# Expert rows with their last 64 channels at both ends, transposed two tiles together

## What is computed

```python
def _L0_ffn_ref(x, gate_w, gate_b, w1, b1, w2, b2):       # 4 experts, 2 of them per token
    probs = softmax(einsum('bsd,de->bse', x, gate_w) + gate_b)
    ...                                                    # mask of the two largest, renormalised
    h = gelu(einsum('bsd,edh->ebsh', x, w1) + b1, approximate=False)     # 192 -> 768
    y = einsum('ebsh,ehd->ebsd', h, w2) + b2                             # 768 -> 192
    out = einsum('bse,ebsd->bsd', masked, y)

x = x + conv_ref(_ln_c(x), ...)
t = _to_tokens(x)
t = t + _L0_ffn_ref(_ln_t(t), ...)
```

## Time and profile before

| | |
|---|---|
| time, median of 3 runs | 1939.6 us (1937.39 to 1943.02) |
| the profiled execution | 1935.69 us, span 1933.5 us |
| busy share of the span | PE 92%, PEld 76%, DVE 74%, ACT 65%, POOL 60% |
| busy tenths of PE in 40 slices | `5999999999987983989999999999999999999946` |
| the same of DVE | `4988999899885576778787887887866755555622` |
| granted clock of PE in tenths (9 is 90% or more) | `9999999999997986999999999999999999999977` |
| DMA share in tenths | `4464533222314896878888788788787877667869` |

### The profile page before, as it was taken

One profiled execution on the slowest core, in us unless ns is written; L12 is line 12 of the kernel. 1 busy time (PEld: TensorE's weight loads), 2 busy tenths in 40 slices (PEclk: granted clock), 3 DMA queues, 4 the chain that ended last, 5 costly groups with the idle time before them and its releaser, 6 DMA issues. The chain is left out here.

```text
span 1933.5 us, 35208 instructions
## 1 busy us (share of the span) xinstructions
PE 1772.1 (92%) x9644; PEld 1460.3 (76%) x9644; DVE 1428.1 (74%) x3470; ACT 1253.0 (65%) x2481; POOL 1158.6 (60%) x1077
## 2 busy tenths in 40 slices
PE   5999999999987983989999999999999999999946
PEld 3666666666655773878888888888899888889934
DVE  4988999899885576778787887887866755555622
ACT  3888888888864431656666666666667666677822
POOL 3777666766661026777777777777676675444310
PEclk9999999999997986999999999999999999999977
DMA  4464533222314896878888788788787877667869
GB/s 100 148 166 130 154 96 96 86 82 81 99 38 134 269 272 219 259 197 237 247 231 237 224 249 249 198 241 225 220 219 192 251 201 199 164 178 180 236 201 335
DMA packets 246671, 364.51 MB, mean 189 GB/s; under 512 B 27620, under 2 KB 178532, under 8 KB 246436
## 3 DMA queue, kind: packets, MB, share of 16 engines
q1 hardware_dynamic: 186500, 286.26, 48.6%
q0 software_dynamic: 50016, 60.00, 15.2%
q10 hardware_dynamic: 9984, 16.26, 2.4%
HBM read 228.83 MB, written 135.73 MB: 189 GB/s over the span
## 5 line engine op out<-in xcount | busy, mean ns | idle before, releaser
L1395 POOL DMA_INDIRECT acc_scratch<-yo,tix x262 | 432.6, 1651 | 274.9 <-DVE yo L1813 168.1
L1976 PE MATMUL bank<-x_all,w1b 128*128 128x512 f32 (+1 forms) x2100 | 542.8, 388 | 1.0 <-ACT hf L1449 1.0
L1993 PE MATMUL bank<-w_hl,hh 128*128 x1572 | 491.6, 363 | 10.6 <-DVE hl L1928 6.4
L1449 ACT ACTIVATE hf<-bank,b_col 128x512 f32<-128x512 f32 (+1 forms) x420 | 277.8, 661 | 317.9 <-PE bank L1976 316.4
L1928 DVE TENSOR_TENSOR hl<-hf,hh 128x512 fp32r<-128x512 f32 (+1 forms) x420 | 274.1, 656 | 220.9 <-ACT hh L1452 219.7
L1994 PE MATMUL bank<-w_hl,hl 128*128 x1572 | 396.8, 252 | 0.0
L1976 PEld LDWEIGHTS bank<-x_all,w1b 128*128 128x128 f32 x2100 | 352.4, 188 | 49.3 <-ACT hf L1449 1.4
L666 DVE SCALAR_TENSOR_TENSOR bank<-zwin,wdw,bank 128x512 f32<-128x512 f32 (+2 forms) x462 | 336.6, 735 | 49.0 <-PE bank L766 40.4
L1380 POOL DMA_INDIRECT xs_scratch<-xn,idx x256 | 297.7, 1163 | 85.1 <-issue 75.0
L1993 PEld LDWEIGHTS bank<-w_hl,hh 128*128 128x128 f32 x1572 | 296.0, 188 | 51.0 <-issue 18.4
L1994 PEld LDWEIGHTS bank<-w_hl,hl 128*128 128x128 f32 x1572 | 299.7, 191 | 16.9
(11 more groups left out here) (267 smaller groups left out, 2901.3 us busy)
## 6 DMA issues: line engine op xcount, KB each, us to landing
w1b<-w1s_scratch SPq DMA_DIRECT2D x140, 768.0 KB, 4.9
xs<-xs_scratch SPq DMA_DIRECT2D x61, 522.0 KB, 6.0
xtok_scratch<-xtok SPq DMA_DIRECT2D x32, 384.0 KB, 2.9
xtok<-xtok_scratch SPq DMA_DIRECT2D x32, 384.0 KB, 6.9
acc_scratch<-x SPq DMA_DIRECT2D x32, 384.0 KB, 6.3
xn<-acc_scratch SPq DMA_DIRECT2D x32, 384.0 KB, 5.7
xc_a<-in_x_dram SPq DMA_DIRECT2D x32, 256.0 KB, 2.7
out_dram<-xs ACTq DMA_DIRECT2D x32, 256.0 KB, 4.7
```

Of the source, the lines that this page charges most:

```text
L1395: nc.gpsimd.indirect_dma_start(acc_dram, bass.IndirectOffsetOnAxis(ap=tix[:, J % 4, t:t + 1], axis=0), yo[:, J % YN, t, :], None, compute_ ...
L1449: nc.scalar.activation(hf[:, k % 3, 0:cols], lb[k % 2][:, 0:cols], ACT.Gelu, bias=b1_col[:, bass.ds(exp_of[J] * CH + k, 1)]).then_inc(gelu, 1)
L1976: last = nc.tensor.matmul(lb[k % 2][:, 0:cols], w[:, q, :], v[:, J % 2, 0:cols], start=(i == 0), stop=(i == 4))
L1993: nc.tensor.matmul(out[:, 0:2 * C], hh[:, k % 3, cols], w, start=(k == 0), stop=False, skip_group_check=True)
```

## The change

The row is laid out anew: the last 64 channels, token number, four gate weights, then all 192 channels (`C0` on). It begins and ends with the same 64 channels and still has 261 numbers. So in a partition of `xs` the end of tile `2a` and the beginning of tile `2a + 1` are 128 neighbouring columns, and one transpose turns the last channels of both: those of the even tile land on partitions 0 to 63, those of the odd one on 64 to 127. `mb[1]` is thus half as wide. ScalarE writes the high part of each half on its own partitions, with one copy for even and one for odd tiles; VectorE writes the rest of each on the other 64 partitions, also in two instructions. Even tiles have the high part on top and odd ones at the bottom, which is the same to the weights.

```diff
-CID, CG = 2 * CA, 2 * CA + 1
-CW = CG + E
+CID, CG = CB, CB + 1
+C0 = CG + E
+CW = C0 + C
...
+            def c_turned(m, t):
+                return mb[1][CB * t:CB * t + CB, 0:64 * m].rearrange("p (a n) -> p a n", n=128)
+            def c_part(J, rows, t):
+                return x_c[rows * CB:rows * CB + CB, J % 2, 0:128 * tiles(J)].rearrange("p (a t n) -> p a t n", t=2, n=128)[:, :, t, :]
...
@@ ScalarE, k == 2
                             act.wait_ge(ac2, 2 * nxt + 2)
-                            nc.scalar.activation(x_c[:, nxt % 2, 0:cols], mb[1][:, 0:cols], ACT.Copy).then_inc(hi2, 1)
+                            for t in (0, 1):
+                                last = nc.scalar.activation(c_part(nxt, t, t), c_turned(tiles(nxt), t), ACT.Copy)
+                            last.then_inc(hi2, 1)
...
-                            nc.scalar.activation(xn[:, s % XN, :, C:CID], xn[:, s % XN, :, CA:C], ACT.Copy)
+                            nc.scalar.activation(xn[:, s % XN, :, 0:CB], xn[:, s % XN, :, C0 + CA:CW], ACT.Copy)
...
@@ VectorE, normalise
-                        last = nc.vector.tensor_scalar(xn[:, s % XN, t, 0:C], x1[:, s % X1N, t, 0:C], mv2[:, s % 2, t, 0:1],
+                        last = nc.vector.tensor_scalar(xn[:, s % XN, t, C0:CW], x1[:, s % X1N, t, 0:C], mv2[:, s % 2, t, 0:1],
...
@@ VectorE, k == 3
-                            nc.vector.tensor_tensor(x_c[CB:128, nxt % 2, 0:cols], mb[1][CB:128, 0:cols], x_c[CB:128, nxt % 2, 0:cols].bitcast(FP32), ALU.subtract)\
-                                .then_inc(lo2, 1)
+                            for t in (0, 1):
+                                last = nc.vector.tensor_tensor(c_part(nxt, 1 - t, t), c_turned(tiles(nxt), t), c_part(nxt, t, t).bitcast(FP32), ALU.subtract)
+                            last.then_inc(lo2, 1)
...
@@ TensorE, turn
-                    for h in (0, 1):
-                        for t in range(tiles(J)):
-                            last = nc.tensor.transpose(mb[h][:, t * 128:t * 128 + 128], xs[:, J % 2, t, h * 128:h * 128 + 128], ident[:, :])
-                        last.then_inc(ac2, 1)
+                    for t in range(tiles(J)):
+                        last = nc.tensor.transpose(mb[0][:, t * 128:t * 128 + 128], xs[:, J % 2, t, C0:C0 + CA], ident[:, :])
+                    last.then_inc(ac2, 1)
+                    flat = xs[:, J % 2, :, :].rearrange("p t c -> p (t c)")
+                    for a in range(tiles(J) // 2):
+                        last = nc.tensor.transpose(mb[1][:, a * 128:a * 128 + 128], flat[:, (2 * a + 1) * CW - CB:(2 * a + 1) * CW + CB], ident[:, :])
+                    last.then_inc(ac2, 1)
```

More of the change, by code:

```diff
@@ L1316, in _ @@
                             sp.dma_start(xs_dram[r:r + TOK, :].rearrange("(p t) c -> p t c", t=ROWS), zrow[:, :, :]).then_inc(st_pad, 16)
-                        sp.dma_start(acc_dram[DUMP:DUMP + TOK, :].rearrange("(p t) c -> p t c", t=ROWS), zrow[:, :, 0:C]).then_inc(st_pad, 16)
+                        sp.dma_start(acc_dram[DUMP:DUMP + TOK, :].rearrange("(p t) c -> p t c", t=ROWS), zrow[:, :, C0:CW]).then_inc(st_pad, 16)
                     if n == n_a - 2:
@@ L1667, in gate @@
                     linked()
-                    nc.vector.tensor_tensor(xn[:, (b % 2) * BATCH:(b % 2) * BATCH + BATCH, :, CG:CW].rearrange("p s t e -> p (s t) e"),
+                    nc.vector.tensor_tensor(xn[:, (b % 2) * BATCH:(b % 2) * BATCH + BATCH, :, CG:C0].rearrange("p s t e -> p (s t) e"),
                                             pm, per_tile(rden), ALU.mult).then_inc(gate_ok, 1)
```

## The result

The changed kernel took 1928.07 us (median of 10 runs, 1922.42 to 1934.41), the kernel before, timed beside it, 1938.4 (median of 10). The ratio is 0.9937, 95% interval 0.9925 to 0.9949: a gain of 12.2 us by the ratio (10.3 by the medians), where the forecast had 8.9 and 1930.7 us. The direction was right and the time lies in the range; by the ratio the size was 3.3 us short. Where those come from is the question of this part.

The account below looks back on a forecast made before the run. TensorE was taken to bound the kernel from 900 to 1840 us. Full turns -11.0, gate beats +1.0, stall +0.2, half beats +1.0 and ninth turn -0.1 gave -8.9 us, so 1930.7 us; range 1926.5 to 1937.5 us.

Parts of the forecast that it names:

- The price of 0.108 from start to start: TensorE's turns: each transpose removed saves 0.108 us, so 0.215 us per full block and 0.108 us per half block.
- neither 0.09 nor 0.133: TensorE's turns: lower and upper bounds in us for one transpose, giving -9.2 and -13.6 us over 51 turns.
- Rivals 1 and 2: Split instructions as dear as whole ones, 1937.6 us, chance 0.10; GpSimd and DMA rings set the pace, 1939.6 us, 0.11.
- The gain stays whole: Ordinary full blocks: 0.99 us free before hl is needed, 0.49 us eaten, so the full 0.215 us is kept.
- the 9.9 of the sum: The 61 full blocks: gain in us from ordinary turns -11.0, gate beats +1.0, stall +0.2, ninth turn -0.1.
- the forecast had 0.19 each: Gate beats: VectorE sets their length, so each of five grows by 0.19 us, +1.0 us in all.
- the third rival: Gate beats: longer TensorE stalls bring the granted clock down, costing 17 us, 1948 us in all; chance 0.07.
- the stall: Start of the blocks: TensorE stands 5.86 us until 845.77; earlier turns' gain is lost there and +0.2 us added.
- The forecast had +0.13 us: Half blocks: TensorE stalls 0.24 us for hl, having saved 0.11, so each beat grows by 0.13 us.
- the upper bound of the forecast: ScalarE's split copy: 0.18 us added if the second copy starts only when the first is through; 0.08 was taken.
- So from 900 to 1840 us an instruction that TensorE no longer issues is time off the span: Expert blocks: TensorE, busy 855.2 of 862.0 us in full and 77.3 of 78.0 in half blocks, sets the time.
- eight half beats x 0.13 = +1.0: Half blocks: the sum's term for eight beats, each longer by 0.13 us, adding 1.0 us to the time.

Follow-up runs that it names:

- experiment 2: The kernel before with the copy and the subtraction of the last channels each cut into even and odd tiles, transposes unchanged: 1938.53 us, ratio 0.9992.
- experiment 7: The kernel before with one, then two added VectorE subtractions that nothing reads, in half blocks alone: 1942.05 us (ratio 1.0005) and 1938.43 us (0.9996).
- experiment 5: The kernel before and the changed one, half-block results written to own arrays without waiting for earlier adds: 1928.78 us (ratio 0.9949) and 1923.3 us (0.9911).
- experiment 6: The changed kernel with joined transposes in ordinary full blocks only, then also half blocks, then half blocks alone: 1930.87 us (0.995), 1929.66 us (0.995), 1938.63 us (0.9992).

## Why the prediction was right, and where it was wrong

**Right: the bound of the full blocks, and what a transpose is worth.** Ordinary beats are 0.21 to 0.22 us shorter (14.95 to 14.74), 0.79 to 0.57 in the turn. The price of 0.108 from start to start held to the hundredth; neither 0.09 nor 0.133 would have fitted. `hl` of the fourth chunk stays ahead by 0.76 us in the beat of the earlier trace rows (block 29), where it had 1.14, so it lost 0.38 where 0.49 was reckoned. The least margin of a full block outside the gate beats is 0.62, in a beat behind a gate's. Rivals 1 and 2 fall by this: no full beat outside the gate beats waits for `hl`, and the wait for rows, where it comes at all, takes 0.2 to 1.9 us in one beat and does not stand in for the turns.

**Overlooked, though it nearly cancels: the wait for VectorE's output.** "The gain stays whole" was argued from the margin of `hl` alone. In the third chunk of a beat TensorE also waits, bank by bank, for VectorE to put out the block before. In the beats of blocks 12, 20 and 28, two behind a gate's, this wait took the gain: they are 0.06 to 0.08 us longer (15.35 to 15.41 in block 12), not 0.215 shorter, which is 0.9 us in all. Block 12, before and then changed:

```profile
993.21 0.74 DVE L1813 SCALAR_TENSOR_TENSOR yo<-bank,wt,yo 128x192 f32<-128x192 f32 x2
...
993.67 0.44 PE L1993 MATMUL bank<-w_hl,hh 128*128 x1
```

```profile
996.54 0.73 DVE L1824 SCALAR_TENSOR_TENSOR yo<-bank,wt,yo 128x192 f32<-128x192 f32 x2
...
997.01 0.44 PE L2005 MATMUL bank<-w_hl,hh 128*128 x1
```

Counted from the start of the chunk (991.60 and 994.65), that matmul comes 2.07 us in before and 2.36 after. Against it stands the beat of block 44, which gained 0.52. So the 9.9 of the sum for the full blocks met the measured 9.3 to 10.0 in part by cancellation.

**Right: the gate beats.** The two subtractions and what follows (compare):

```profile
1235.70 0.86 DVE L1932 TENSOR_TENSOR x_all<-bank,x_all 64x256 fp32r<-64x256 f32 x2
...
1236.59 0.17 DVE L1806 COPY wt<-xs 128x4 f32 x1
...
1237.58 0.44 PE L2005 MATMUL bank<-w_hl,hh 128*128 x1
...
1239.83 0.41 PE L2047 MATMUL bank<-msk,tri_s 128*128 128x64 f32 x2 [0.86 <-DVE msk L1663]
```

0.89 us for 0.73. VectorE sets the length of these beats, and four of the five grew by 0.15 to 0.19, the first by 0.36; the forecast had 0.19 each. The wait for the mask is 0.86 for 0.83, and the granted clock stayed at 1.00 from 860 to 1830 us, so the third rival falls too. The beat ahead of the stall grew by 0.15 and that of the stall by 0.24 (forecast 0.2 in all); the latter lies within what one and the same kernel shows, for it took 26.31 and 26.41 us in the two traces of before and 26.41 to 26.65 in the three of the changed kernel:

```profile
844.66 1.43 DVE L1618 TENSOR_SCALAR xn<-x,mv,rstd 128x192 f32<-128x192 f32 x4 [6.44 <-POOL rstd L1412]
...
849.66 0.68 PE L2005 MATMUL bank<-w_hl,hh 128*128 x1 [6.02 <-DVE hl L1940]
```

6.02 us of idle time for 5.86. The rule on instructions of different quadrants (the Trainium skill, "VectorE: DVE Perf Modes", section "Two Vector instructions with no wait between them") is borne out: the two crossing subtractions of 64x256 start 0.43 us apart and last 0.42 and 0.43, so they did not overlap, and the pair cost 0.15 us more than one of 64x512. The pair of experiment 2, on its own partitions, lasts as long but starts 0.35 us apart, and cost 0.07 more.

**Mis-sized: the half beats.** The forecast had +0.13 us, the trace has 7.42 to 7.70, +0.28 where nothing else disturbs. A half block (compare):

```profile
1795.41 0.54 ACT L1529 ACTIVATE x_all<-bank 64x128 fp32r<-64x128 f32 x2
...
1796.44 0.59 DVE L1932 TENSOR_TENSOR x_all<-bank,x_all 64x128 fp32r<-64x128 f32 x2
...
1797.06 0.17 DVE L1806 COPY wt<-xs 128x2 f32 x1
...
1797.21 0.96 DVE L1940 TENSOR_TENSOR hl<-hf,hh 128x256 fp32r<-128x256 f32 x2
...
1797.78 0.44 PE L2005 MATMUL bank<-w_hl,hh 128*128 x1
```

The two small copies on ScalarE took 0.54 us where one took 0.38: 0.16 and not 0.08. So the upper bound of the forecast, that the second copy starts when the first is through, was the true value, for 256 columns (0.76 for 0.59) as for 128. In number the fixed part that the Trainium skill gives ScalarE ("VectorE: DVE Perf Modes", section "The TRN2 errata — SBUF-src ops pay a fixed extra latency per instruction"), which I had weighed at 0.14 us and set aside, was nearer than my 0.08. But experiment 2 speaks against it as the cause: there two copies of 256 columns on the same partitions start 0.26 us apart and cost 0.07 more than one, while here the second goes to the other 64 partitions and starts 0.38 us after the first, which takes 0.36. What the two runs differ in is this move to other partitions, which the forecast considered for VectorE alone. VectorE kept its two for 0.62 in place of 0.46, 0.16 and not 0.19. Together with the shorter turn that leaves TensorE 0.19 us later at the fourth second-layer group, counted from the start of the turn; and the first matmul after the wait took 0.44 where 0.34 is usual, a tenth more that the sum did not have.

**Wrong: what the half beats are worth.** The step that failed is "So from 900 to 1840 us an instruction that TensorE no longer issues is time off the span", with "after 1840 us the loads of the sums; both stay as they are". From block 61 on it is the chain of adds, and the busy TensorE of the earlier trace rows hid it: 77.3 of 78.0 us say that it had work, not that its work was last. The term "eight half beats x 0.13 = +1.0" is nearly +2 by its true size (seven beats of 0.28; the first half beat stayed at 9.05), and is worth nothing in the time: nearly 6 us of the same kind (seven times 0.83) cost nothing that could be measured (experiment 7). With the chain taken away the stretch does grow by it (61.21 to 63.17, experiment 5). The sum then reads -9.6 us, the full blocks of the first trace alone: 1930.0 us in place of 1930.7. This is the step that is known to have failed; it explains 1 us of the 3.3, less the 0.3 by which the full blocks fell short.

**Open: 2 us.** The mean of three comparisons is 11.6 us and their lowest 8.9; -9.6 lies between the two. The kernel before measured against itself gave 2.3 us. So what the change is worth beyond the measured full blocks is not shown, and that the first comparison fell within the range is in part luck. Traces show where such scatter sits: the start of block 0 at 777.2 to 781.2 and block 61 to the last add at 77.0 to 83.5 us for one and the same changed kernel. Whether a part of the 2 us is a real gain in the chain of adds these runs do not settle, and its cause stays open. The distance from the last result to the last add was 3.3, 6.2, 6.5, 8.0 and 9.1 us in the five traces with half beats of 7.7 us and 7.1 to 9.9 in the seven with half beats of 7.4 to 7.6, which looks like one, but the timed runs of experiment 6 are too coarse to show it.

## What to carry to other kernels

A full engine is the bound only where its last instruction is what the end waits for. At each change of stage, and above all near the end of the kernel, compare when the last result is ready with when the last one is stored: a distance that one landing does not explain means that a chain has taken over, and then work on the full engine is worth nothing. The distance of starts, taken between groups of different count, gave the price of a transpose to the hundredth of a microsecond; cutting one instruction in two cost 0.07 us on VectorE and on ScalarE where both halves stayed on the same partitions, and 0.15 to 0.17 where the second half moved to others. That is free only while every consumer has more margin than that, and a full engine can wait for more than one thing in a beat: look at each.

## What was not expected of the hardware

The indirect adds from 1780 us on took 3.5 to 8.2 us from issue to landing (median 5.5) in the trace of before, so that a chain of nine blocks, each waiting for the one before, took 8.0 us a block, more than the computing of 256 rows of an expert (7.42); with plain writes that wait for nothing in its place the kernel took about 10 us less. Two ScalarE copies of 64x256 to different partitions start 0.38 us apart (experiment 2 has 0.26 for two of 128x256 on the same ones), as the two subtractions on VectorE do at 0.43 for 0.35. Behind the waits of TensorE for `hl`, of 0.1 to 0.5 us, the first matmul took 0.43 to 0.44 us and not 0.34, with a granted clock of 1.00. And moving a row's 64 channels to both ends of 261 numbers changed the time no more than could be seen (0.9987 against the 0.9988 of a kernel against itself).
